# High parts of split operands: a mask on VectorE and a copy on ScalarE, or one rounding copy on ScalarE

## The reference, cut to what matters

```
x = layernorm(x + attn(x))      # linear attention, 16 heads of 8: elu(q)+1, elu(k)+1, k / |k|, scores without softmax
x = layernorm(x + xattn(x, c))  # cross attention, 16 heads of 64, 64 context rows a sequence, softmax
x = layernorm(x + ffn(x))       # silu(gate) * up, then down; inputs and weights rounded to blockwise FP4
```

## Time and profile before

| | us |
|---|---|
| median of 3 runs | 373.12 (372.43 to 373.29) |
| span of the profiled execution, first to last instruction | 371.1 |
| median less span | 2.0 |
| PE busy | 349.7 |
| DVE busy | 308.7 |
| POOL busy | 269.0 |
| ACT busy | 253.6 |

### The profile page before, as it was taken

One profiled execution on the slowest core, in us unless ns is written; L12 is line 12 of the kernel. 1 busy time (PEld: TensorE's weight loads), 2 busy tenths in 40 slices (PEclk: granted clock), 3 DMA queues, 4 the chain that ended last, 5 costly groups with the idle time before them and its releaser, 6 DMA issues.

```text
span 371.1 us, 7329 instructions
## 1 busy us (share of the span) xinstructions
PE 349.7 (94%) x2147; PEld 267.9 (72%) x2147; DVE 308.7 (83%) x858; ACT 253.6 (68%) x533; POOL 269.0 (73%) x453
## 2 busy tenths in 40 slices
PE   8999989999998999999999999999999999998774
PEld 7788646675775868787678877786767787887653
DVE  3998557567689998869989779979998998999994
ACT  2957766577676677678688767878767666864553
POOL 4404459958988699969689895898988569784535
PEclk9999999999999999999999999999999999999999
DMA  8900100001000001000000000100000000000010
GB/s 248 305 2 16 30 1 16 14 16 29 15 17 14 17 0 44 28 18 16 29 14 17 14 1 17 31 0 0 17 15 2 15 2 1 15 16 14 3 30 28
DMA packets 13586, 10.44 MB, mean 28 GB/s; under 512 B 971, under 2 KB 12396, under 8 KB 13548
## 3 DMA queue, kind: packets, MB, share of 16 engines
q1 hardware_dynamic: 12540, 7.89, 7.1%
q10 hardware_dynamic: 1008, 2.10, 1.7%
HBM read 7.88 MB, written 2.10 MB: 27 GB/s over the span
## 4 chain that ended last, share of the span: by engine, by line
PE 70%; DVE 9%; POOL 8%; issue 6%; ACT 4%; DMA 1%; SPq 0%; POOLq 0%; DVEq 0%
PE A L2892 13%; PE S L2862 12%; PE TP L2852 7%; PE F L2916 6%; PE TP L2880 6%; PE A L2936 5%; PE S L2871 3%; PE A L2813 2%; PE TP L2791 2%; POOL pe L440 2%; PE F L2791 2%; PE S L2791 2%; PE TP L2925 2%; PE A L2826 2%; PE A L2821 1%
## 5 line engine op out<-in xcount | busy, mean ns | idle before, releaser
L440 POOL TENSOR_TENSOR pe<-pe,srec 128x1024 f32<-128x1024 f32 x32 | 60.9, 1904 | 9.2 <-DVE srec L1860 8.9
L2862 PE MATMUL S<-M,x1T 128*128 128x512 f32 x128 | 60.7, 597 | 1.5 <-ACT pe L1076 1.4
L2892 PEld LDWEIGHTS A<-wvoT,wqkT 128*128 128x128 f32 x480 | 56.4, 192 | 3.1 <-issue 1.8
L2892 PE MATMUL A<-wvoT,wqkT 128*128 128x128 f32 x480 | 58.0, 276 | 0.1
L434 POOL TENSOR_TENSOR fold<-pe 128x512 f32<-128x512 f32 x32 | 40.9, 1277 | 14.6 <-ACT pe L1076 14.4
L1843 DVE TENSOR_REDUCE smax<-S 128x16 fp32r<-128x1024 f32 x32 | 38.7, 1211 | 3.3 <-PE S L2862 3.1
L1076 ACT ACTIVATE pe<-S 128x1024 f32<-128x1024 f32 x32 | 32.6, 1019 | 10.6 <-PE S L2871 10.3
L1081 ACT ACTIVATE wqkT<-TP 128x1024 f32<-128x1024 f32 x32 | 32.6, 1018 | 4.3 <-PE TP L2880 4.1
L2862 PEld LDWEIGHTS S<-M,x1T 128*128 128x128 f32 x128 | 22.2, 190 | 18.3 <-issue 15.3
L2916 PE MATMUL F<-w_gu_r,GT 128*128 128x352 f32 x168 | 35.1, 344 | 0.1
L2880 PE MATMUL TP<-ident,pe 128*128 128x128 f32 x256 | 33.5, 274 | 1.6 <-POOL pe L440 0.9
(11 more groups left out here) (247 smaller groups left out, 888.2 us busy)
## 6 DMA issues: line engine op xcount, KB each, us to landing
xT<-in_x_t SPq DMA_DIRECT2D x16, 128.0 KB, 2.2
x_sb<-in_x SPq DMA_DIRECT2D x16, 128.0 KB, 2.2
out<-yf SPq DMA_DIRECT2D x15, 128.0 KB, 1.8
M<-in_fw SPq DMA_DIRECT2D x1, 560.0 KB, 11.0
wqkT<-in_wq_t ACTq DMA_DIRECT2D x2, 256.0 KB, 4.6
wqkT<-in_wk_t ACTq DMA_DIRECT2D x2, 256.0 KB, 6.1
ctx_f<-in_ctx_t ACTq DMA_DIRECT2D x2, 256.0 KB, 7.0
wvoT<-in_wv_t ACTq DMA_DIRECT2D x1, 512.0 KB, 9.4
```

The lines of the kernel that those rows point to most:

```text
L440: ge.tensor_tensor(w, w, spread(srec[n % NFO][:, :], HX, R), ALU.mult).then_inc(pn_made, 1)
L2862: last = te.matmul(S[:, half * BANK:half * BANK + BANK], x1T[b % 2][:, t * P:t * P + P], M[:, b // BH, HC * half:HC * half + HC, b % BH * ...
L2892: last = te.matmul(part(A2, t), pT[n % 2][:, j, :], vo[b % 2][:, j, :], start=(j == 0 and b not in SUM_ON_PE), stop=(j == NJ - 1))
```

## The change

The cuts on DVE are gone (23 instructions: two of the context, four of G, two of the weights, fifteen of the input), with their tiles and semaphores. ACT's copy reads the full value, from PSUM (G, input) or SBUF (context, weights), and writes it into the fp32r tile, which rounds it. The low part is the full value minus what ACT wrote, so it waits for ACT's copy. The four functions change alike; here two of them and the two that make the low parts:

```diff
             def g_keep_high(half, par):
-                k = 2 * half + par
-                act.wait_ge(g_cut, k + 1)
-                sc.activation(g_tile(half, par)[0], high_bits[2 + k].rearrange("p (a b) -> p a b", a=4),
+                act.wait_ge(g_made, half + 1)
+                sc.activation(g_tile(half, par)[0], G_BANKS[half][par].rearrange("p (a b) -> p a b", a=4),
                               ACT.Copy).then_inc(g_high, 1)
...
             def gate_up_low(m):
-                pool.wait_ge(gu_cut_made, m + 1)
-                ge.tensor_tensor(w_gu_r[:, 1, m, :], w_gu[:, m, :], gu_cut[m], ALU.subtract).then_inc(gu_low_made, 1)
+                pool.wait_ge(gu_high_made, m + 1)
+                ge.tensor_tensor(w_gu_r[:, 1, m, :], w_gu[:, m, :], w_gu_r[:, 0, m, :].bitcast(FP32), ALU.subtract).then_inc(gu_low_made, 1)
...
-                    act.wait_ge(xf_cut_made, b + 1)
-                    sc.activation(xf_r[b % 2][:, 0, :], xf_cut[:, :], ACT.Copy).then_inc(xfT_kept, 1)
+                    act.wait_ge(xfT_made, b + 1)
+                    sc.activation(xf_r[b % 2][:, 0, :], A2[:, 0:T * P], ACT.Copy).then_inc(xfT_kept, 1)
...
-            def xf_cut_high(b):
-                dve.wait_ge(xfT_made, b + 1)
-                wait_free(dve, xfT_kept, b)
-                ve.tensor_scalar(xf_cut[:, :].bitcast(INT32), A2[:, 0:T * P].bitcast(INT32), HIGH_MASK, None,
-                                 ALU.bitwise_and).then_inc(xf_cut_made, 1)
-
             def xf_keep_low(b):
-                dve.wait_ge(xf_cut_made, b + 1)
-                ve.tensor_tensor(xf_r[b % 2][:, 1, :], A2[:, 0:T * P], xf_cut[:, :], ALU.subtract).then_inc(xf_low_made, 1)
+                dve.wait_ge(xfT_kept, b + 1)
+                ve.tensor_tensor(xf_r[b % 2][:, 1, :], A2[:, 0:T * P], xf_r[b % 2][:, 0, :].bitcast(FP32), ALU.subtract).then_inc(xf_low_made, 1)
```

More of the change, by code:

```diff
@@ L167, in decoder_layer @@
         fw_m, fw_s, fw_r = (hT[1][:, 0, NWB * k:NWB * k + NWB] for k in range(3))
-        gu_cut = [w[:, 1, 0:I] for w in hT]
-        high_bits = [w[:, 512 * k:512 * k + 512] for w in pe_ for k in range(2)]
         A1, A2, S, TP, F = banks("A1", 1), banks("A2", 1), banks("S", 2), banks("TP", 2), banks("F", 2)
@@ L207, in decoder_layer @@
         bias_made = sem("bias_made")
-        c_cut, c_high, c_low = sem("c_cut"), sem("c_high"), sem("c_low")
-        g_made, g_cut, g_high, g_low = sem("g_made"), sem("g_cut"), sem("g_high"), sem("g_low")
+        c_high, c_low = sem("c_high"), sem("c_low")
+        g_made, g_high, g_low = sem("g_made"), sem("g_high"), sem("g_low")
         m_made = sem("m_made")
@@ L234, in decoder_layer @@
         xfT_made, xfT_kept = sem("xfT_made"), sem("xfT_kept")
-        xf_cut_made, xf_low_made = sem("xf_cut_made"), sem("xf_low_made")
-        gu_cut_made, gu_high_made, gu_low_made = sem("gu_cut_made"), sem("gu_high_made"), sem("gu_low_made")
+        xf_low_made = sem("xf_low_made")
+        gu_high_made, gu_low_made = sem("gu_high_made"), sem("gu_low_made")
         gu_made, th_made, hg_made, h_made = sem("gu_made"), sem("th_made"), sem("hg_made"), sem("h_made")
@@ L403, in context_low @@
             def context_low(half):
-                pool.wait_ge(c_cut, half + 1)
+                pool.wait_ge(c_high, half + 1)
                 cols = slice(512 * half, 512 * half + 512)
-                ge.tensor_tensor(ctx_r[:, 1, cols], ctx_f[:, cols], high_bits[half], ALU.subtract).then_inc(c_low, 1)
+                ge.tensor_tensor(ctx_r[:, 1, cols], ctx_f[:, cols], ctx_r[:, 0, cols].bitcast(FP32), ALU.subtract).then_inc(c_low, 1)
             def gate_up_low(m):
-                pool.wait_ge(gu_cut_made, m + 1)
-                ge.tensor_tensor(w_gu_r[:, 1, m, :], w_gu[:, m, :], gu_cut[m], ALU.subtract).then_inc(gu_low_made, 1)
+                pool.wait_ge(gu_high_made, m + 1)
+                ge.tensor_tensor(w_gu_r[:, 1, m, :], w_gu[:, m, :], w_gu_r[:, 0, m, :].bitcast(FP32), ALU.subtract).then_inc(gu_low_made, 1)
             def x_plus_rows(b):
@@ L960, in context_high @@
             def context_high(half):
-                act.wait_ge(c_cut, half + 1)
-                sc.activation(ctx_r[:, 0, 512 * half:512 * half + 512], high_bits[half], ACT.Copy).then_inc(c_high, 1)
+                act.wait_ge(ctx_loaded[half], 16)
+                cols = slice(512 * half, 512 * half + 512)
+                sc.activation(ctx_r[:, 0, cols], ctx_f[:, cols], ACT.Copy).then_inc(c_high, 1)
             def g_keep_high(half, par):
-                k = 2 * half + par
-                act.wait_ge(g_cut, k + 1)
-                sc.activation(g_tile(half, par)[0], high_bits[2 + k].rearrange("p (a b) -> p a b", a=4),
+                act.wait_ge(g_made, half + 1)
+                sc.activation(g_tile(half, par)[0], G_BANKS[half][par].rearrange("p (a b) -> p a b", a=4),
                               ACT.Copy).then_inc(g_high, 1)
@@ L995, in gate_up_high @@
             def gate_up_high(m):
-                act.wait_ge(gu_cut_made, m + 1)
-                sc.activation(w_gu_r[:, 0, m, :], gu_cut[m], ACT.Copy).then_inc(gu_high_made, 1)
+                act.wait_ge(fwT_kept, m + 1)
+                sc.activation(w_gu_r[:, 0, m, :], w_gu[:, m, :], ACT.Copy).then_inc(gu_high_made, 1)
             def k_exp(b):
@@ L1715, in biases @@
                                  ALU.subtract).then_inc(bias_made, 1)
[L1717 to L1725, removed]
             def g_keep_low(half, par):
                 k = 2 * half + par
-                dve.wait_ge(g_cut, k + 1)
+                dve.wait_ge(g_high, k + 1)
                 ve.tensor_tensor(g_tile(half, par)[1], G_BANKS[half][par].rearrange("p (a b) -> p a b", a=4),
-                                 high_bits[2 + k].rearrange("p (a b) -> p a b", a=4), ALU.subtract).then_inc(g_low, 1)
+                                 g_tile(half, par)[0].bitcast(FP32), ALU.subtract).then_inc(g_low, 1)
             def m_keep(half, hd):
@@ L2048, in _ @@
             k_guess(0)
-            context_cut(1)
             m_keep(0, 1)
@@ L2073, in _ @@
             m_keep(1, 5)
-            gate_up_cut(0)
             keep_kvT(0)
@@ L2077, in _ @@
             m_keep(1, 7)
-            gate_up_cut(1)
             k_sums(2)
@@ L2229, in _ @@
             statistics("post", 5)
-            xf_cut_high(1)
             xf_keep_low(1)
@@ L2267, in _ @@
             statistics("attn", 6)
-            xf_cut_high(2)
             k_guess(9)
@@ L2318, in _ @@
             q_features(8)
-            xf_cut_high(3)
             keep_kvT(8)
@@ L2329, in _ @@
             statistics("ffn", 2)
-            xf_cut_high(4)
             xf_keep_low(4)
@@ L2524, in _ @@
             score_max(11, 0)
-            xf_cut_high(8)
             xf_keep_low(8)
@@ L2572, in _ @@
             score_max(12, 1)
-            xf_cut_high(9)
             xf_keep_low(9)
@@ L2585, in _ @@
             score_max(13, 0)
-            xf_cut_high(10)
             xf_keep_low(10)
@@ L2676, in _ @@
             gate_times(12, 0)
-            xf_cut_high(13)
             gated(12, 0)
@@ L2696, in _ @@
             h_rounded_up(12)
-            xf_cut_high(14)
             h_rounded(12)
```

16 lines of the change are left out of this document (removed).

## The result

| | before | after |
|---|---|---|
| median, us (4 runs each) | 372.97 (372.43 to 373.29) | 380.54 (379.65 to 380.95) |
| span of the profiled execution | 371.1 | 379.1 |
| mean granted TensorE clock | 0.999 | 0.992 |

The ratio is 1.0201, with a 95% interval from 1.0188 to 1.0213. The time lies in the range of the prediction (374.6 to 382.3) and 2.3 us above its centre.

What follows compares the result with a forecast made beforehand. PE and what it waits for, not DVE, was taken as the bound. Span 371.1 + 2.0 (to the median) + 2.7 (G) + 0.5 (context, weights) + 1.5 (inputs) + 0.4 (tail) = 378.2 us; range 374.6 to 382.3.

Steps and rivals of the forecast that it cites:

- What bounds the kernel: Whole kernel: PE holds 70% of the chain, DVE 9%; shorter DVE work moves nothing unless PE waits for it.
- Durations: ACT's copies from PSUM: 0.38 us for each input, 0.60 for each of G's, taken from similar copies.
- Head, G's parts (+2.7): Start of kernel: G's low parts wait for ACT's copies, PE's third product 2.7 us later, range 2.0 to 3.2.
- Weights through POOL's queue (+0.5): Head: POOL's second weight low part waits for ACT's copy, delaying batch 0's layer norm 1.1 us; 0.5 taken, from 0 to 1.1.
- The fifteen inputs (+1.5): Batches 0 to 14: low parts 7.8 us later in all, 2.4 hitting PE ahead of the tail; 1.5 taken.
- Tail (+0.4): After 325 us, where DVE leads: low parts of batches 12 to 14 shift; +0.4 us, from -0.8 to +0.8.
- Relief decides: Rival: the fifteen input masks saved on DVE come off the end, 6.2 us, giving 370.1 us; chance 0.08.
- Head alone: Rival: only G's parts cost, 2.7 us; waits in batches and POOL's queue are made good, 375.9 us; chance 0.18.
- Waits pile up: Rival: all 7.8 us of later input low parts reach the end, giving 384.1 us; chance 0.08.
- The marks: Signs expected in the profile: product starts near 13.6 and 16.95, 3 us late at 50 us, longer waits by DVE and PE.

Runs made afterwards that it cites:

- relief run: Kernel before without the fifteen input masks and with no new wait; copy and low part read the untransposed tile xv: 372.60 us, ratio 0.9995.
- run with the head alone: Kernel before with the change made only for context, G and weights; the fifteen inputs keep their masks: 375.18 us, ratio 1.0068.
- reordered head: Changed kernel with all four high parts of G as early in ACT's list as ACT can make them: 377.12 us, ratio 1.0115.
- inputs' run: Kernel before with only the fifteen input masks removed; context, G and weights keep theirs: 377.35 us, ratio 1.0123.

## Why the prediction was right, and where it was mis-sized

- **What bounds the kernel.** Right: PE and what it waits for, not DVE. The relief run shows it directly (0.9995 for 6.2 us of DVE).
- **Durations.** Right: from PSUM to fp32r, ACT took 0.38 for the inputs and 0.58 to 0.60 for G, the 0.38 and 0.60 that were taken from copies of the same shapes. The busy time of ACT fell, so it isn't the copies that cost.
- **Head, G's parts (+2.7).** The waits were right step by step: the run with the head alone has the third product 2.47 later and 2.4 us in the time, and the reordered head has nothing of it. What was not in the sum is the clock. In the profile of after 0.54 us between the first and the third product go with it; the medians leave 0.5 us that neither half has (7.57 less 7.05), which may be that in part. This isn't shown.
- **Weights through POOL's queue (+0.5).** POOL's `nmean_attn` came at 39.83 instead of 35.29, 1.1 later than the 3.43 that all had by then, exactly the delay worked out for it. But PE's step there was 0.20 in that profile, and with the head alone PE's product at 40 us is no later than the third product of M (2.39 against 2.47). The value lay in the middle of its bounds, and the lower one was right.
- **The fifteen inputs (+1.5).** The term that failed in size: 3.9 came (7.55 less 3.63). The direct hits had been found: 0.45, 0.4, 0.5, 0.3, 0.7 and 0.1 at batches 1, 2, 4, 7, 8 and 10, against 0.43, 0.35, 1.10, 0.28, 0.64 and 0.25 measured. Two mistakes followed. First, 0.9 of the 2.4 was taken off since "some of it will be made good"; nothing was. PE has no idle time there in which to make it good, and its later waits are, as I read them, for what hangs on its own products and so comes later with them; no run tests that by itself. Second, only waits of PE for the low part itself were counted. At batch 11 PE doesn't wait for it at all, as predicted, but DVE does:

```profile
307.54 0.42 DVE L1875 TENSOR_TENSOR GT<-A,GT 128x256 fp32r<-128x256 f32 x1 [1.76 <-ACT GT L1088]
...
309.46 1.22 DVE L1823 TENSOR_REDUCE smax<-S 128x16 fp32r<-128x1024 f32 x1
...
310.73 0.30 PEld L2822 LDWEIGHTS S<-smax,ident_r 128*128 128x128 f32 x2 [0.46 <-DVE smax L1823]
```

  The maximum stands some calls behind the low part in DVE's list, and PE waits for that: 0.52 us here, 0.35 more at 307 us through the `hv` chain, and 0.6 of batch 4's 1.10 in the same way. These 1.5 us are the rest of the gap.
- **Tail (+0.4).** 0.57. Right in kind and size.
- **The rivals.** Relief decides: refuted by the relief run. The Trainium skill, "Perfetto Trace Analysis", section "Optimizing Scalar/DVE Operations", speaks of moving work from a saturated vector engine to ScalarE; this case isn't quite what it speaks of, since DVE was at 83% and ACT got no new instruction. What the runs show is narrower: taking 6.2 us from DVE gave nothing, since PE didn't wait for it. Head alone: refuted by the inputs' run (+4.6). Waits pile up (+7.8 for the inputs): 3.9 of the 7.8 us reached the end.
- **The total.** Head and weights were put at 3.2 us and cost 2.4; inputs and tail were put at 1.9 and cost 4.6; 0.5 is in neither. The inputs' 3.9 lie above the 3.3 with which the upper end of the range was formed. That the time still lay inside is in part luck: the head came in low.
- **The marks.** The first and the third product came at 13.88 and 17.88 where 13.6 and 16.95 were named (13.27 and 16.73 with the head alone), and at 50 us all was 3.6 us late where 3 were named. PE's weight loads waited 2.4 us for the low part, against 0.7 before, inside the 2 to 3 named. DVE waited 18.2 us (11.9 and 6.3) for ACT's copies of GT, where 5 to 8 had been named: I had set only the lateness of the low parts, not the masks' time that turned into waiting.

## What to carry to other kernels

When an operation is taken away that let two engines start side by side, look at the order of the list in which the remaining one stands: here one changed wait cost 5.9 us, the operations saved gave nothing where no wait was added, and moving eleven calls in ACT's list gave back 6.8 of 7.6. On a path where the bounding engine has no idle time, add up every delay in full, the ones through a second engine's queue too, and take nothing off for slack that no row shows. And where two calls of one engine are already wanted at once, a third may leave no order in which nobody waits; of the six orders here three were tried, and none was free.

## What the runs showed of the hardware

- ACT's copy into fp32r takes 380 ns for 128x256 from PSUM against 414 from SBUF, and 590 to 599 for 128x512 against 620. Copies of the same shapes from PSUM into f32 take 381 and 589 to 599, so writing fp32r costs nothing to be seen.
- PE idle for most of 13 to 14 us, after another idle stretch from 11 to 12, was followed by a granted clock of 0.50 in the profile of after. In the run with the head alone similar waits left it at 1.00 (ahead of `project_q(0)` and of the first product of M, PE idle for 0.9 and 1.0 us there, for 1.3 and 1.0 in after). Which of two such executions loses the clock stays open; it was worth 0.9 us on six matmuls (2.57 against 1.65).
- The very first products of a launch start at a time that differs from execution to execution: the first product of G at 6.42 to 7.30 us in the profiles of kernels whose lists for PE don't differ up to there. Ahead of it PE works off 26 warm-up products. In before the last of them take 275 ns each instead of 421; in after none takes less than 421, and PE comes to G's product later. The two rows (count, busy us, mean ns) are for the first 9 us of before and of after:

```profile
L2980 PE MATMUL A<-fold 128*128 128x128 f32 x26 | 5.0, 376 | 1.5 <-POOL fold L380 1.5
L2931 PE MATMUL A<-fold 128*128 128x128 f32 x26 | 5.9, 427 | 1.5 <-POOL fold L375 1.5
```

  That alone moves profiled spans by some tenths, and asks for medians where less than 1 us is at stake.
